# Routed layers with the first product turned, latent projections in half-precision pairs, and biases loaded ahead of the expert weights

## What is computed

```python
x = x + L0_xattn(ln(x), ctx, ...)   # attention with a 3x3 convolution over the scores
x = x + L0_ffn(ln(x), ...)          # quantised gate/up/down
x = x + L1_xattn(ctx, ln(x), ...)   # latent attention, 16 heads of 64
x = x + L1_ffn(ln(x), ...)          # routed: 8 experts, one per token, relu, capacity 320
x = x + L2_xattn(ln(x), ctx, ...)
x = x + L2_ffn(ln(x), ...)          # all experts, gated
x = x + L3_xattn(ln(x), ctx, ...)
x = x + L3_ffn(ln(x), ...)          # routed: 8 experts, one per token, gelu, biases b1, b2
```

```python
# L1_xattn, per batch: latents are the 1024 tokens, x the 77 context tokens
ln = layernorm(latents) * ln_l_g + ln_l_b
xn = layernorm(x) * ln_x_g + ln_x_b
q  = ln @ Wq                                   # 256 -> 1024
k, v = split(concat([xn @ Wkv, ln @ Wkv]))     # 256 -> 2 * 1024
qn = q / max(norm(q per head) / 8, 1e-8) * qn_g / 8
kn = k / max(norm(k per head) / 8, 1e-8) * kn_g
out = softmax(qn @ kn.T) @ v @ Wout + bout
# L3_ffn (L1_ffn has relu, no biases and a capacity)
probs = softmax(x @ gate_w); e = argmax(probs)
out   = probs[e] * (gelu(x @ w1[e] + b1[e]) @ w2[e] + b2[e])
```

## Time and profile before

| | us |
|---|---|
| median of 3 runs | 3793.15 (3786.95 to 3793.6) |
| the profiled execution, its own time | 3791.13 |
| its span in the profile | 3789.5 |
| mean granted clock of TensorE | 0.879 |
| busy: PE, PEld, DVE, ACT, POOL | 3069.7, 2065.3, 2093.1, 1880.0, 1214.8 |

### The profile page before, as it was taken

The page is one execution under the profiler, slowest core; times in us unless marked ns, Lnnn a source line. Parts: engine busy times, 40 slices in busy tenths (PEclk is TensorE's granted clock), DMA queues, the critical chain, the costliest instruction groups (busy, mean ns, idle before and its releaser), DMA issues. The chain is left out here.

```text
span 3789.5 us, 67756 instructions
## 1 busy us (share of the span) xinstructions
PE 3069.7 (81%) x25908; PEld 2065.3 (54%) x25909; DVE 2093.1 (55%) x3119; ACT 1880.0 (50%) x2854; POOL 1214.8 (32%) x877
## 2 busy tenths in 40 slices
PE   3979997634869998879997595967999999893595
PEld 2756665314436666436666464664666666572474
DVE  3968885495557873558783223745444444482121
ACT  2438885251338785338884011644555555372131
POOL 1239995000008884017873102630000000071102
PEclk7769998767879999889998797877999999996698
DMA  2421111000012220012222411000011000146111
GB/s 68 160 82 54 56 54 37 33 0 12 0 29 48 59 49 9 0 30 60 52 51 104 147 33 41 8 28 23 23 33 36 23 23 1 37 89 214 48 33 61
DMA packets 225403, 184.70 MB, mean 49 GB/s; under 512 B 135667, under 2 KB 185120, under 8 KB 224608
## 3 DMA queue, kind: packets, MB, share of 16 engines
q1 hardware_dynamic: 219838, 166.31, 15.5%
q0 software_dynamic: 5280, 14.42, 1.1%
HBM read 107.75 MB, written 35.59 MB: 38 GB/s over the span
## 5 line engine op out<-in xcount | busy, mean ns | idle before, releaser
L2212 POOL TENSOR_TENSOR lta_p_lo<-lta_p,lta_p_hi 128x1024 f16<-128x1024 f32 x256 | 539.0, 2134 | 528.2 <-DVE lta_p_hi L2335 528.2
L2407 ACT ACTIVATE lta_p<-lta_banks,lt_gmax 128x512 f32<-128x512 f32 x512 | 323.8, 683 | 113.4 <-PE lta_banks L2250 108.9
L2318 DVE TENSOR_REDUCE lta_s_ps<-lta_s_ps 128x1 f32<-128x1101 f32 x240 | 314.3, 1310 | 106.9 <-PE lta_s_ps L2229 106.9
L3397 PE MATMUL m2e_h_ps<-m2e_x,m2e_w 128*128 128x512 f16 x1536 | 353.7, 380 | 22.2 <-DVE m2e_w L3502 19.0
L3409 PE MATMUL m2e_y_ps<-m2e_w,m2e_hT 128*128 128x256 f16 x3072 | 355.6, 273 | 0.0
L3507 DVE TENSOR_TENSOR m2e_hT<-m2e_h,m2e_hT 128x512 f16<-128x512 f32 x256 | 177.3, 693 | 298.3 <-ACT m2e_hT L3450 296.6
L3450 ACT ACTIVATE m2e_h<-m2e_h_ps,m2e_h_bias,m2e_h_scale 128x512 f32<-128x512 f32 x256 | 199.2, 778 | 281.5 <-PE m2e_h_ps L3397 258.5
L3409 PEld LDWEIGHTS m2e_y_ps<-m2e_w,m2e_hT 128*128 128x128 f16 x3072 | 300.5, 98 | 61.5 <-issue 0.5
L985 POOL TENSOR_TENSOR c0a_tri_p_lo<-c0a_tri_p,c0a_tri_p_hi 128x1024 f16<-128x1024 f32 (+2 forms) x192 | 285.6, 1521 | 62.3 <-DVE c0a_tri_p_hi L1158 61.4
L3397 PEld LDWEIGHTS m2e_h_ps<-m2e_x,m2e_w 128*128 128x128 f16 x1536 | 150.5, 98 | 179.6 <-DVE m2e_w L3502 19.7
L1229 ACT ACTIVATE c0a_tri_p<-c0a_banks,c_size 128x512 f32<-128x512 f32 (+3 forms) x384 | 208.4, 576 | 46.8 <-PE c0a_banks L1053 35.9
(11 more groups left out here) (724 smaller groups left out, 6624.6 us busy)
## 6 DMA issues: line engine op xcount, KB each, us to landing
m_w<-in_L_ffn_w_dram SPq DMA_DIRECT2D x4, 8192.0 KB, 43.0
m_raw<-in_L_ffn_W_dram SPq DMA_DIRECT2D x16, 1024.0 KB, 6.4
lta_q<-ltb_qT SPq DMA_DIRECT2D x96, 128.0 KB, 2.4
c_side<-in_fside_Bx16xSxS_dram SPq DMA_DIRECT2D x16, 616.0 KB, 4.8
c0a_tri_q<-c_near SPq DMA_DIRECT2D x96, 96.0 KB
c0a_tri_k<-c_mixed SPq DMA_DIRECT2D x96, 96.0 KB
lta_k<-ltb_kT SPq DMA_DIRECT2D x64, 137.6 KB, 2.5
lt_vh<-ltb_v SPq DMA_DIRECT2D x64, 128.0 KB
```

Source lines behind the costliest of these rows:

```text
L2212: nc.gpsimd.tensor_tensor(p_lo[:, slot, :], p32[:, p32_slot(h, j), :], p_hi[:, slot, :], ALU.subtract).then_inc(rested, 1)
L2318: nc.vector.tensor_reduce(ntop_of(h)[:, n:n + 1], scores(h, n), AX_X, ALU.max, negate=True).then_inc(top_ready, 1)
L2407: nc.scalar.activation(p32[0:rows, slot, c * 512:(c + 1) * 512], t_ps[0:rows, c, :], ACT.Exp, bias=bias, scale=p["gmax"][0:rows, 0:1]).the ...
L3397: last = nc.tensor.matmul(h_ps[:, f % RING, :], w1[:, v, a, c, f * P:(f + 1) * P], x16[:, b, c, n * CHUNK:(n + 1) * CHUNK], start=c == 0 a ...
```

## The change

Six things change.

1. `routed_experts`: the first product is turned. Slices of 128 x 128 of `w1` are the stationary operand and the turned tile is the moving one, so that the result has the hidden channels in the partitions and needs no transposes. 16 products of 128 columns stand for 4 of 512. DVE copies the expert's `w1` (128 x 2048 in float32) to `w_mine` ahead of it, and takes over the copy `xT`; ACT applies the function straight from `h_ps`. `hT` and `y_ps` get a second buffer. PE runs `expand` one tile ahead and `turn_x` two.
2. `route_tokens`: `b1` is loaded as 64 rows of 128 contiguous elements, and with `b2` ahead of the zeros and the weights; PE turns the rows in one transpose behind the router's products and ACT copies them.
3. `combine_experts` of the last layer stores each tile of `x` as soon as it is added; `store_stage` is gone.
4. `LatentWeights` and `latent_norms`: the weights are scaled and split into float16 pairs (six pieces of 128 x 1024, the rounded part on ACT, the rest on DVE) in place. Gains and shifts are loaded spread over all partitions. The pair of `Wout` goes to DRAM, and `latent_emit` loads it for each batch.
5. `latent_project`: gain and shift move to POOL, the tile becomes a float16 pair (ACT and POOL), four float16 transposes stand for two in float32, and each product is three float16 products (pairs without rest times rest).
6. `latent_project`: queries and keys have norms, roots, waits and scalings of their own (semaphores by side), the steps of one tile are laid over four turns of a list, and all is written out without a loop.

```diff
-        self.wq, self.wkv = st.sb("wq", [P, DC, INNER]), st.sb("wkv", [P, DC, 2 * INNER])
+        self.room = st.sb("room", [P, LatentWeights.LEAD + 3 * DC, INNER])
...
@@ latent_norms
-                sp.dma_start(p["affine"][:, k, :], w(n).rearrange("(c p) -> p c", p=P), allow_slow_non_contiguous=True).then_inc(loaded, 16)
+                sp.dma_start(raw_affine[:, k, :], w(n).partition_broadcast(P)).then_inc(loaded, 16)
...
+            sp.wait_ge(wo_halved, 1)
+            sp.wait_ge(wo_split, 1)
+            sp.dma_start(p["wo"], wo16[:]).then_inc(wo_stored, 16)
+            sp.wait_ge(wo_stored, 16)
...
+            for k in range(LatentWeights.PIECES):
+                dve.wait_ge(w_halved, k + 1)
+                nc.vector.scalar_tensor_tensor(weights.half(k, 1), weights.raw(k), w_scale, weights.half(k, 0), ALU.mult,
+                                               ALU.subtract).then_inc(w_split, 1)
...
@@ latent_project, TensorE
+        def product(dst, n, pieces, half):
             rows = rows_of(n)
             for c in range(DC):
-                last = nc.tensor.transpose(x_ps[:, c * P:c * P + rows], turn[0:rows, u, c * P:(c + 1) * P],
-                                           env.ident[0:rows, 0:rows])
+                for x, y in TERMS:
+                    last = nc.tensor.matmul(dst, lT[:, n % 2, x, c, 0:rows], weights.half(pieces[c], y)[:, half * HALF:(half + 1) * HALF],
+                                            start=c == 0 and (x, y) == TERMS[0], stop=c == DC - 1 and (x, y) == TERMS[-1])
+            return last
...
@@ latent_project, VectorE: one turn of the list
+        for s in range(STEPS):
+            if within(s):
+                normalise(s)
+            if within(s - 3):
+                rest(s - 3, K, 1)
+            if within(s - 2):
+                sums(s - 2, K)
+            if within(s - 2, Q):
+                split_values(s - 2, 1)
+            if within(s - 2):
+                invert(s - 2, K)
...
@@ latent_emit
+        sp.dma_start(wo16[:], p["wo"]).then_inc(wo_loaded, 16)
         sp.dma_start(bout[:], w("bout").partition_broadcast(P)).then_inc(loaded, 16)
...
@@ route_tokens
+        if b1 is not None:
+            sp.dma_start(b1_rows[:], w("b1").rearrange("e (c p) -> (e c) p", p=P)).then_inc(rows_loaded, 16)
+            sp.dma_start(b2[:], w("b2").partition_broadcast(P)).then_inc(weights_loaded, 16)
         sp.wait_ge(zero_made, 1)
...
         sp.dma_start(w2[:], w("w2").rearrange("e (c p) d -> p e c d", p=P)).then_inc(weights_loaded, 16)
-        if b1 is not None:
-            sp.dma_start(b1[:], w("b1").rearrange("e (c p) -> p e c", p=P), allow_slow_non_contiguous=True).then_inc(weights_loaded, 16)
-            sp.dma_start(b2[:], w("b2").partition_broadcast(P)).then_inc(weights_loaded, 16)
...
@@ routed_experts, TensorE
         def expand(j, u):
-            e = pe.value_load(expert_of[0:1, bass.ds(j, 1)], min_val=0, max_val=E - 1)
+            pe.wait_ge(w_copied, j + 1)
             pe.wait_ge(x_evac, j + 1)
-            for k in range(HB):
+            for f in range(FC):
                 for c in range(DC):
-                    last = nc.tensor.matmul(h_ps[:, u, k * 512:(k + 1) * 512], xT[:, u, c, :],
-                                            w1[:, bass.ds(e, 1), c, k * 512:(k + 1) * 512].rearrange("p a n -> p (a n)"),
+                    last = nc.tensor.matmul(h_ps[:, u, f * P:(f + 1) * P],
+                                            w_mine[:, u, c, f * P:(f + 1) * P], xT[:, u, c, :],
                                             start=c == 0, stop=c == DC - 1)
             last.then_inc(h_done, 1)
...
@@ routed_experts, VectorE
+        def copy_w(j, u):
+            e = dve.value_load(expert_of[0:1, bass.ds(j, 1)], min_val=0, max_val=E - 1)
+            if not (isinstance(j, int) and j < 2):
+                dve.wait_ge(h_done, j - 1)
+            nc.vector.tensor_copy(w_mine[:, u], w1[:, bass.ds(e, 1), :, :].rearrange("p a c n -> p (a c) n")).then_inc(w_copied, 1)
...
@@ combine_experts of the last layer
+            for t in range(TILES):
+                sp.wait_ge(added, t + 1)
+                sp.dma_start(rows[:, t, :], env.x[:, t, :]).then_inc(stored, 16)
+            sp.wait_ge(stored, 16 * TILES)
```

More of the change, by code:

```diff
@@ L2018, in halve @@
+        def halve(n, k, half):
             rows = rows_of(n)
-            for half in range(2):
-                act.wait_ge(turned, 2 * side_at(n, k) + (half + 1))
-                dst = (qT, kT)[k][:, 0, half * 4:(half + 1) * 4, bass.ds(n * P, rows)]
-                nc.scalar.activation(dst, t_ps[:, half * 512:(half + 1) * 512].rearrange("p (c t) -> p c t", c=4)[:, :, 0:rows],
-                                     ACT.Identity, scale=1.0 if k == 0 else p["gain"][:, 0:1]).then_inc(halved, 1)
@@ L2041, in _ @@
-        affine(0, 0, False)
-        for k in range(2):
-            square(0, k)
-        affine(1, 1, False)
-        root(0)
-        for k in range(2):
-            halve_values(0, k)
-        tiles(act, work)
+            act.wait_ge(turned[k], 2 * n + half + 1)
+            dst = (qT, kT)[k][:, 0, half * 4:(half + 1) * 4, n * P:n * P + rows]
+            nc.scalar.activation(dst, t_ps[:, half * HALF:(half + 1) * HALF].rearrange("p (c t) -> p c t", c=4)[:, :, 0:rows],
+                                 ACT.Identity, scale=1.0 if k == Q else p["gain"][:, 0:1]).then_inc(halved[k], 1)
@@ new lines, in turn_side @@
+        def turn_side(n, k, half):
+            rows = rows_of(n)
+            pe.wait_ge(scaled[k], n + 1)
+            if k == K and n < LAST:
+                pe.wait_ge(rested[Q], 2 * n + half + 1)
+            elif n:
+                pe.wait_ge(rested[K], 2 * n - 2 + half + 1)
+            for c in range(4 * half, 4 * half + 4):
+                last = nc.tensor.transpose(t_ps[:, c * P:c * P + rows], qk[0:rows, k, c * P:(c + 1) * P], env.ident[0:rows, 0:rows])
+            last.then_inc(turned[k], 1)
@@ L2679, in of_buffer, with tiles @@
         return 8 * j + (16 - 8 * u)
-    def pipeline(eng, front, back):
-        front(0, 0)
-        with eng.Fori(0, (NT - 1) // 2) as i:
-            for v in range(2):
-                front(2 * i + (1 + v), 1 - v)
-                back(2 * i + v, v)
-        back(NT - 1, (NT - 1) % 2)
+    def tiles(eng, work):
+        for j in range(2):
+            work(j, j)
+        with eng.Fori(1, (NT - 3) // 2) as i:
+            for u in range(2):
+                work(2 * i + u, u)
+        for j in range(NT - 3, NT):
+            work(j, j % 2)
+    within = lambda j, ahead: not isinstance(j, int) or j + ahead < NT
     @block.sync
@@ L2709, in store @@
             nc.gpsimd.dma_start(sorted_y[bass.ds(j * P, P), :], ys[:, u, :]).then_inc(ys_stored[u], 16)
[L2711 to L2714 removed]
+        tiles(pool, store)
         pool.wait_ge(ys_stored[0], 16 * ((NT + 1) // 2))
@@ L2809, in back, with combine_experts @@
                                         ALU.add).then_inc(y_evac, 1)
-        pipeline(dve, front, back)
-def combine_experts(nc, env, st, ctx, sorted_y, slot, weight):
+        dve.wait_ge(weights_loaded, 32 if b1 is None else 48)
+        for j in range(2):
+            copy_w(j, j)
+            keep_x(j, j)
+        tiles(dve, work)
+def combine_experts(nc, env, st, ctx, sorted_y, slot, weight, out):
     yg = st.sb("yg", [P, TILES, D])
     gathered = env.gathered.pop()
-    added = st.sem("added")
+    added, stored = st.sem("added"), st.sem("stored")
```

599 lines of the change are left out of this document (304 added, 295 removed).

## The result

| | before | after |
|---|---|---|
| median of the runs, us | 3790.05 (3786.24 to 3793.6, 4 runs) | 3632.69 (3631.52 to 3637.15, 4 runs) |
| the profiled execution, its span | 3791.13, 3789.5 | 3631.52, 3629.9 |

The ratio is 0.9587, with a 95% interval of 0.9571 to 0.9604: 157 us less, where 155 were forecast (3638, range 3616 to 3680). Later runs were made beside the kernel before on other chips (3786 to 3787 there), so runs are compared by their ratio to it; the kernel after stands at 3630 on that scale. Five of them (`two_terms`, `four_terms`, `half_width`, `rows_last`, `elements_first`) have one execution each, and are read mainly by the stages in their traces.

A forecast was written before the change was run, and what follows sets the result against it. Bounds: PE's work plus DVE stalls and half clock in the projection, PE's work in the experts, SP's queue before the last experts. 3791.1 - 40 - 39 - 95 + 21 + 5 - 6.5 = 3636.6, median 3638, range 3616 to 3680.

The forecast's parts named there:

- Projection: Latent projection, both batches: half-precision products and separate norms cut the tile period from 16.7 to 10.5 us; 95 us gained.
- The full clock in the steady part: Latent projection: with PE busy 94% of the period, the full clock was expected, where the mean was 0.88.
- 2 us for the longer fill: Latent projection, per batch: POOL's passes before the first product and two more list turns take 2 us off the gain.
- Turned product: Routed experts, both layers: without the eight transposes a tile falls to 7.19 us, at 0.11 per record; 39 us gained.
- Biases first: Last routed layer, ahead of its experts: the two late bias issues cost 41.2 us, their replacements 1.2; 40 us gained.
- Norms: Latent norms: splitting weights and storing the pair of Wout add 21 us, bounds 17 and 25.
- reload: latent_emit: the first product now waits for the 1 MB load of Wout's pair; 5 us added for two batches.
- output: Kernel's end: with a store per tile only the last 128 KB follow the last addition; 6.5 us gained.
- Loads in line: Rival, turned product: each weight load adds to its stream, a tile takes 10.7 us, total 3802; chance 3%.
- The persisting half clock: Rival, projection: half clock and stall stay, period 12.2 to 13 us, total 3665 to 3678; chance 20%.
- The gainless projection: Rival, projection: nothing gained beyond the stall, period 14.9 us, +70, total 3708; chance 4%.
- wrong in kind: Sign against the forecast: DVE waits for ACT in every projection tile, or PE waits for `w_mine`.

The follow-up runs named there:

- two_terms: Kernel after, with the product of activation rest and rounded weights left out in the latent projection, two half-precision products for three; 3619.9 us.
- four_terms: Kernel after, with a fourth half-precision product, rest times rest, added to each product of the latent projection; 3670.4 us.
- half_width: Kernel after, with every 128-column product of the experts' first product made as two of 64 columns, in both routed layers; 3818.4 us.
- rows_last: Kernel after, with b1 still as 64 contiguous rows and b2 spread, but issued behind w1 and w2 in the last routed layer; 3661.7 us.
- elements_first: Kernel after, with b1 loaded as 8192 separate elements, still ahead of the zeros and weights, without PE's transpose and ACT's copy; 3645.0 us.

## Why the prediction was right, by its steps

- **Projection, -95, measured -98.8.** The period was 10.29 for 10.5. The number was near, the engine was wrong, and that the two came so close was luck: DVE's work was 1.1 us too high, a sum of durations that overlap, and PE's 9.75 and a wait of 0.54 that I had not seen gave nearly the same. The full clock in the steady part came as forecast. A cost of 6.3 us in the first batch, POOL's first addition, was missing from my "2 us for the longer fill". The better period (16 tiles x 0.2 = 3) and a fill shorter than I thought made up for it: -45.4 and -53.4 for the batches, where I had 47.6 each.
- **Turned product, -39, measured -38.5.** Record 0.112 for 0.11, tile 7.25 for 7.19. The reading of the earlier trace rows, that the 0.114 is not the stream and hides it, is what `half_width` showed; that it is the load is still my reading. DVE's copy was over-priced twofold, without effect.
- **Biases first, -40, measured -38.7.** Right by the difference of two stages. The reason that the forecast gave for `b2`'s 8.45 us, `b1`'s elements ahead of it, held. For `b1`'s 33 us I had given no reason; they come with the place behind 16 MB, not with the number of elements.
- **Norms +21, measured +20.1; reload +5, measured +4.0; output -6.5, measured -6.1.** The store took 4.8 where I had 6.2, and DVE's chain was 1.2 longer than I had.
- **The rivals.** Loads in line are refuted by the 0.111 of 64 columns. The persisting half clock is refuted by 1.00 in the window from 985 to 1065; a small wait did persist. The gainless projection would have had a period of 14.9. I had written that I would be wrong in kind if DVE waited for ACT in every tile of the projection. It does, by 0.21 us:

```profile
1023.42 1.22 DVE L1951 TENSOR_REDUCE ltp_ss<-ltp_sq 128x16 f32<-128x1024 f32 x1 [0.21 <-ACT ltp_sq L2038]
```

It costs nothing there, since PE's chain is the longer one. But the same kind of handing over between engines, PE to ACT and back, is in the 0.54 us of PE, so the sign pointed at something real. PE does not wait for `w_mine` in the experts.

## To carry to other kernels

When two engines are each near 95% busy, the period doesn't say which is the limit; lengthen and shorten one of them, and add up distances between starts, not durations. Issue small loads ahead of large ones on a queue: behind 16 MB of weights a load of 32 KB held its engine for 32 to 33 us in either form, and ahead of them for under 0.6 (5.5 with the next issue, where the load was in separate elements). In float32 turn a product as long as the moving side stays at 128 columns or more, for a record of 64 costs the same 0.11 us.

## What the runs showed of the hardware that I had not expected

- DVE's copy of 128x2048 float32 in SBUF, and the same with rounding to half precision, takes 1.23 us; the two-input operation of that size takes 2.29 to 2.35.
- A float32 record of 64 columns costs 0.111 at the full clock and 0.217 at half clock, so the floor of such a record goes with TensorE's clock.
- The first elementwise instruction of POOL behind the norms' reduction over partitions begins 6.9 us late, once, even with 8 columns.
- A half-precision record of 65 columns costs 0.031 us at the full clock, a float32 one 0.114.
- PE, busy with float32 records of 64 columns, stayed at half clock for 30 us, in both layers.
